# An attention layer with a gated output: eight exponential buffers, a pair's first values one batch later, and filler shared by TensorE's whole batch

## What is computed

```python
xn = layernorm(x)
q, k, v = (xn @ wq.T + bq) * D**-0.5, xn @ wk.T + bk, xn @ wv.T + bv     # by head
s = softmax(q @ k.T + causal_mask) @ v                                   # by head
s = s @ wo.T + bo
g = silu(xn @ weight.T + pooled(xn) @ disha)      # pooled: sums over groups of 64 columns
out = x + s * g
```

## Time and profile before

| | |
|---|---|
| median of 3 runs | 582.64 us (582.53 to 584.64) |
| the profiled execution | 583.26 us |
| its slowest core's span | 581.7 us; the eight cores 575.6 to 581.7 us |
| TensorE busy | 519.4 us, 89% |
| ScalarE busy | 398.0 us, 68% |
| VectorE, GpSimd busy | 222.9 us, 122.1 us |

### The profile page before, as it was taken

The page is one execution under the profiler, slowest core; times in us unless marked ns, Lnnn a source line. Parts: engine busy times, 40 slices in busy tenths (PEclk is TensorE's granted clock), DMA queues, the critical chain, the costliest instruction groups (busy, mean ns, idle before and its releaser), DMA issues.

```text
span 581.7 us, 9555 instructions; the slowest of 8 cores (575.6 to 581.7 us)
## 1 busy us (share of the span) xinstructions
PE 519.4 (89%) x2688; PEld 207.9 (36%) x2688; DVE 222.9 (38%) x335; ACT 398.0 (68%) x495; POOL 122.1 (21%) x157
## 2 busy tenths in 40 slices
PE   2889989889979898899999999999998998999896
PEld 1334433333324343333333333433342333333242
DVE  4447566455311230452022212113110635545625
ACT  2256667767655876787688887677748887888650
POOL 0433332221110211011011111010100332252215
PEclk9989999999989999999999999999999999999899
DMA  7933244043111110111010103110205222223113
GB/s 167 282 105 103 91 145 146 19 154 119 37 37 36 38 55 0 55 38 36 1 38 1 42 32 107 39 37 37 74 0 163 72 91 75 91 73 109 61 50 146
DMA packets 17488, 43.68 MB, mean 75 GB/s; under 512 B 2336, under 2 KB 2336, under 8 KB 17056
## 3 DMA queue, kind: packets, MB, share of 16 engines
q1 hardware_dynamic: 17440, 43.07, 23.7%
HBM read 34.67 MB, written 8.39 MB: 74 GB/s over the span
## 4 chain that ended last, share of the span: by engine, by line
PE 62%; ACT 14%; issue 11%; DVE 8%; DMA 3%; POOL 1%; ACTq 0%; SPq 0%; DVEq 0%; POOLq 0%
PE PSF L556 34%; PE PSS L568 10%; PE PSO L586 10%; ACT PT L732 9%; PE PSO L588 7%; DVE QA L696 2%; DVE QA L695 2%; DMA xfirst<-x 2%; DMA wo_sb<-wo 1%; ACT Rb L742 1%; ACT Rb L741 1%; ACT Rb L744 1%; DVE Vp L638 1%; DVE QA L655 1%; PE PSS L556 1%
## 5 line engine op out<-in xcount | busy, mean ns | idle before, releaser
L732 ACT ACTIVATE PT<-PSS,neg 128x1024 f16<-128x1024 f32 (+1 forms) x320 | 299.3, 982 | 110.0 <-PE PSS L568 106.7
L761 POOL TENSOR_TENSOR PT<-PT,tri_sb 128x256 f16<-128x256 f16 x128 | 88.2, 699 | 424.8 <-ACT PT L732 421.0
L556 PE MATMUL PSF<-XG,wqk 128*128 128x512 f16 x512 | 126.2, 383 | 3.9 <-DVE Vp L638 2.2
L586 PE MATMUL PSO<-PT,Vp 128*128 128x512 f16 (+1 forms) x320 | 111.5, 353 | 11.2 <-DVE QA L696 8.9
L568 PE MATMUL PSS<-QA,KT 64*128 64x512 f16 (+3 forms) x640 | 99.4, 353 | 24.4 <-ACT PT L732 17.7
L588 PE MATMUL PSO<-PT,Vp 128*128 128x512 f16 (+1 forms) x320 | 108.9, 350 | 0.0
L556 PEld LDWEIGHTS PSF<-XG,wqk 128*128 128x128 f16 x512 | 49.0, 98 | 58.6 <-issue 7.0
L638 DVE TENSOR_TENSOR Vp<-PSF,bvb 128x512 f16<-128x512 f32 x32 | 22.1, 691 | 117.7 <-PE PSF L556 117.6
L556 PE MATMUL PSF<-wv_sb,XG 128*128 128x512 f16 x256 | 65.9, 384 | 1.1 <-DVE Vp L638 0.7
L568 PEld LDWEIGHTS PSS<-QA,KT 64*128 64x128 f16 x640 | 27.3, 93 | 109.2 <-issue 107.9
L649 DVE TENSOR_SCALAR KT<-PSF,bqk 128x512 f16<-128x512 f32 x32 | 24.0, 750 | 92.4 <-PE PSF L556 92.1
(11 more groups left out here) (39 smaller groups left out, 268.4 us busy)
## 6 DMA issues: line engine op xcount, KB each, us to landing
wqk<-wqk SPq DMA_DIRECT2D x32, 512.0 KB, 3.4
xin<-x SPq DMA_DIRECT2D x24, 256.0 KB, 3.2
out<-esb SPq DMA_DIRECT2D x24, 256.0 KB, 2.0
wbuf<-wT SPq DMA_DIRECT2D x16, 256.0 KB, 3.3
wv_sb<-wv SPq DMA_DIRECT2D x2, 1024.0 KB, 12.3
wo_sb<-wo SPq DMA_DIRECT2D x1, 2048.0 KB, 8.7
out<-elast SPq DMA_DIRECT2D x8, 256.0 KB, 2.4
xfirst<-x SPq DMA_DIRECT2D x4, 256.0 KB, 4.8
```

What stands on the lines that cost most here:

```text
L556: ins = pe.matmul(ps(n), l, r, start=ec == 0, stop=ec == ECH - 1)
L586: pe.matmul(PSO[:, 0, off:512], Vp[:, sc, p, 0:128], PT[u % 6][:, 0, off:512], start=first, stop=last)
L732: act.activation(PT[u % 6][:, :, off:512], PSS[:, 2 * t[2]:2 * t[2] + 2, off:512], AF.Exp, bias=neg2[:], scale=0.125).then_inc(s_exp, 1)
L761: pool.tensor_tensor(a, a, tri2, ALU.mult).then_inc(s_mask, 1)
```

## The change

- `PT` has eight buffers, `wqk` two; `elast` lies in `QA` alone, and the waits of the `XB` tokens on GpSimd go with it.
- `PV`: in stage 0 none in a pair's first batch and two in its second. In the later stages one, one, none, two in the first four batches, then one each.
- `LNK` stands behind the batch's second exponential; `NRM` is due 2.6 us after it.
- Filler is given so that a batch's own work on TensorE plus its filler is in proportion to its exponentials, with 1.8 us more for the batch before whose exponentials `LNK` stands. `BOUNDARY` is gone; `QUOTA` is unchanged.
- A transpose is put behind up to three tiles so that it ends a batch's filler.

```diff
+                if q[0][0] == "T" and count - done > 3 and put_off[0] < 3 and q[1][0] in "KQV":
+                    q[0], q[1] = q[1], q[0]
+                    put_off[0] += 1
+                    continue
...
                     whole(*w)
-                    done += 2
-                    continue
+                    put_off[0] = 0
+                    return done + 2
...
+    def due_values(tc, i):
+        if tc == 0:
+            return 2 if i == 1 and lag[0] != lag[-1] - 1 else 0
+        return (1, 1, 0, 2)[i] if i < 4 else 1
...
-            act = [sum(0.22 + 2 * (512 - off) * 0.83e-3 for _, _, off in bs[b][2]) for b in mine]
-            extra = 0 if before[0] < 0 else ECH if before in GATES else min(BOUNDARY, 0.45 * max(quota, 0))
-            share = [max(quota - extra, 0) * a / sum(act) for a in act]
+            cols = [sum(512 - off for _, _, off in bs[b][2]) for b in mine]
+            act = [0.44 + 2 * c * 0.83e-3 for c in cols]
+            if before[0] >= 0:
+                act[2 if tc else 0] += 1.8
+            former = [sum(512 - off for _, _, off in bs[b][2]) for b in lag]
+            if tc:
+                did = [former[0], former[1], 0, cols[0] + cols[1]] + cols[2:-2]
+            else:
+                did = [0, sum(former)]
+            own = [c / 2400 + 2 * d / 2400 + 0.2 for c, d in zip(cols, did)]
+            extra = ECH if before in GATES else 0
+            span = sum(own) + MM_US * max(quota - extra, 0)
+            share = [max(span * a / sum(act) - o, 0) for a, o in zip(act, own)]
...
-                if len(lag) > 2:
+                for _ in range(due_values(tc, i)):
...
-                    end = values(lag.pop(0))
+                    end = values(lag.pop(0)) or end
                 order.append(("E", b, 1))
+                if end:
+                    sums(*end)
-                if tc == 3 and (p, i) in ((3, 3), (4, 0), (4, 5), (5, 2), (5, 6), (6, 3), (6, 6), (7, 3)):
+                if tc == 3 and p >= 4 and i in (1, 4):
                     order.append(("XB",) + xb.pop(0))
```

More of the change, by code:

```diff
@@ L106, in evict @@
         order.append(("EV", n) + tiles[n])
-        if kind == "Q" and tiles[n][1] * 8 + tiles[n][2] + 3 < 32:
-            order.append(("WQK", tiles[n][1] * 8 + tiles[n][2] + 3))
+        if kind == "Q" and tiles[n][1] * 8 + tiles[n][2] + 2 < 32:
+            order.append(("WQK", tiles[n][1] * 8 + tiles[n][2] + 2))
         if tiles[n] == ("Q", 3, 7):
@@ L222, in values, with sums @@
         advance(sum(2 * (512 - off) for _, _, off in units) / 2400)
[L223 to L229, removed]
+        return (tc, p) if units[1][1] == 4 * tc + 3 else None
+    def sums(tc, p):
+        k = tc * 8 + p
+        order.append(("LNK", k))
+        if k < 31:
+            later(2.6, "NRM", k)
+    def due_values(tc, i):
+        if tc == 0:
+            return 2 if i == 1 and lag[0] != lag[-1] - 1 else 0
+        return (1, 1, 0, 2)[i] if i < 4 else 1
     xb = [(tt, h) for tt in range(12, 16) for h in range(2)]
@@ L240, in schedule @@
             quota = QUOTA[tc][p] - over
-            act = [sum(0.22 + 2 * (512 - off) * 0.83e-3 for _, _, off in bs[b][2]) for b in mine]
             before = (tc, p - 1) if p else (tc - 1, 7)
-            extra = 0 if before[0] < 0 else ECH if before in GATES else min(BOUNDARY, 0.45 * max(quota, 0))
-            share = [max(quota - extra, 0) * a / sum(act) for a in act]
+            cols = [sum(512 - off for _, _, off in bs[b][2]) for b in mine]
[11 more added lines that the diff above has]
+            share = [max(span * a / sum(act) - o, 0) for a, o in zip(act, own)]
+            share = [x * max(quota - extra, 0) / max(sum(share), 0.01) for x in share]
             due_by, emitted = 0.0, 0
@@ L249, in schedule @@
                 order.extend([("S", b), ("E", b, 0)])
-                advance(sum(512 - off for _, _, off in units) / 2400 + 0.2)
+                advance(cols[i] / 2400 + 0.2)
                 lag.append(b)
                 end = None
-                if len(lag) > 2:
+                for _ in range(due_values(tc, i)):
                     c, r, old = bs[lag[0]]
@@ L279, in schedule @@
         order.append(("MM", n, 0, ECH - 1))
-    values(lag.pop(0))
+    sums(*values(lag.pop(0)))
     for n in last[2:4]:
@@ L341, in build_program @@
     o_wqk = used
-    wqk = [at(f"wqk{i}", [NP, 2, ECH, NP], F16) for i in range(3)]
+    wqk = [at(f"wqk{i}", [NP, 2, ECH, NP], F16) for i in range(2)]
     o_PT = used
-    PT = [at(f"PT{i}", [NP, 2, 512], F16) for i in range(6)]
+    PT = [at(f"PT{i}", [NP, 2, 512], F16) for i in range(8)]
     Rb = [at(f"Rb{i}", [NP, 512], F32) for i in range(2)]
@@ L367, in build_program @@
     xlast = [at(f"xlast{i}", [NP, E], F16, o_wqk + 2048 * i) for i in range(4)]
-    elast = [at(f"elast{i}", [NP, 512], F32, o_wqk + 8192 + 2048 * i if i < 2 else o_QA + 2048 * (i - 2))
-             for i in range(8)]
+    elast = [at(f"elast{i}", [NP, 512], F32, o_QA + 2048 * i) for i in range(8)]
     tlast = [at(f"tlast{i}", [NP, 512], F32, o_PT + 2048 * i) for i in range(6)]
@@ L403, in build_program @@
         s_wo = sem("s_wo")
-        s_wqk = [sem(f"s_wqk{i}") for i in range(3)]
+        s_wqk = [sem(f"s_wqk{i}") for i in range(2)]
         s_wt = [sem(f"s_wt{i}") for i in range(2)]
@@ L443, in sync_program @@
             sp.dma_start(out=tri[:], in_=tri_d).then_inc(s_tri, 16)
-            for c in range(3):
+            for c in range(2):
                 sp.dma_start(out=wqk[c][:], in_=wqk_d[c].rearrange(
@@ L548, in tensor_program @@
                         elif kind == "K":
[L549 removed]
+                            l, r = wqk[(8 * i + j) % 2][:, 0, ec, :], keys(i, ec)
                         elif kind == "Q":
[L551 removed]
+                            l, r = wqk[(8 * i + j) % 2][:, 1, ec, :], keys(i, ec)
                         elif kind == "G":
```

26 lines of the change are left out of this document (13 added, 13 removed).

## The result

The changed kernel takes 594.33 us (median of 4 runs, 593.29 to 596.66) where the kernel before takes 582.64 beside it: a ratio of 1.0195, 95% interval 1.0149 to 1.0241. Forecast were 578.5 us and a range of 567 to 588, so both the direction and the range were wrong.

A forecast was written before the change was run, and what follows sets the result against it. TensorE's work plus some 65 us of its waits was taken to bound the kernel. 25.5 us taken away, 21.0 added and 0.5 of clock turned 583.26 into 579.3, so a median of 578.5 us; range 567 to 588.

The forecast's parts named there:

- (j): TensorE's clock: half a stretch more at 1.2 GHz behind new waits on the slowest core, +0.5 us.
- (b): Scores waiting for exponentials in stages 1 to 3: the new filler shares take away 8 us of 25.4.
- (i): Loads into two `wqk` buffers land in time: 0 us, at most 0.7 once; gate bursts also 0.
- (e): Tiles in the filler wait for a bank, their evictions blocked behind `NRM`, in stages 1 to 3: 10.9 us added.
- (a): A pair's first values, now two batches later, no longer wait for the former pair's normalisation: all 11 us go.
- (c): Stages 0 and 1: a tile straight behind a transpose no longer waits for an eviction; gain 4.6 us.
- (d): Stage 0: one score batch no longer stands right behind its projection; gain 1.7 us.
- (f): Transposes wait for their rows: row block 14 in stage 2 3.7 us, two in stage 0 1.4 each; 6.5 added.
- (g): Start of stage 1: first values wait 2.7 us for `NRM`, where 0.43 is found before; net 2.3 added.
- (h): Stage 1: two LayerNorm activations hold exponentials back, the next pair's scores wait 0.65 us each; 1.3 added.
- The rival that stood on it: The clock falls after every long wait: four times 1.7 us, 584 to 585 us; chance 0.07.
- They cost more: Blocked evictions at pair ends cost more, by a later `NRM` or delayed Q tiles; 587 us at 0.8 each; chance 0.22.

The follow-up runs named there:

- shares_old: The changed kernel with the filler shares (`act`, `extra`, `share`) of the kernel before: 605.17 us.
- nrm_late: The changed kernel with `NRM` due 3.7 us behind `LNK` for 2.6 in stages 1 to 3: 583.85 us, ratio to before 0.9981.
- b_wqk2: The kernel before with two of its three `wqk` buffers, each load issued one Q tile later: 586.34 us, ratio to before 0.9993.
- t_pop: The changed kernel with the next row block's LayerNorm statistics listed as soon as a transpose is done: 583.15 us, ratio to before 0.9982.
- t14_late: Changed kernel, `NRM` at 3.4 us, stage 0's last values a batch later, LayerNorm early except in stage 2: 573.80 us; 570.08 with stage 2 early too.

## Why the prediction was wrong, point by point

Two steps failed. (j) put the clock at +0.5 us where it was 6.8. And the waits, forecast 4.5 us down, went 4.6 up: (b) won too little, (i) and the statistics that the put-off moved were set at nothing. The blocked evictions of (e) were right and made the largest cost.

**(a) Values for `NRM`, -11: right.** The earlier trace rows against the waits of after: the 11.3 us are down to 0.5, apart from the start of stage 1. shares_old has none of them either, so the old shares don't bring them back.

**(b) Exponentials, -8: too large.** By the waits view 25.4 became 21.6 (14.8 and 40 times 0.17), by the distances on TensorE 28.5 became 22.4: 4 to 6 us. Stage 2's regular pairs came as forecast (15.15 for 15.1), stage 3's 0.5 longer (20.51 for 20.0), and there are more of them. shares_old shows that the shares do it. The sign named for it, more waits but of 0.2 us, did not come: 40 waits of 0.54 us on average for 45 of 0.56.

**(c) and (d), -6.3: right.** The 0.94 us behind transposes are gone; at one of the five places the tile, now behind scores, still waits 0.5. The scores' 1.7 us are 0 too.

**(e) Blocked evictions, +10.9: right.** 3.0, 3.6 and 1.05 us in pairs 3, 6 and 4 for 2.8, 2.7 and 0.7; 1.3 us at the V tile of stage 2, 0.75 at a V tile in pair 0 of stage 1 for 0.9; the waits of the two gate tiles grew from 0.6 us to 1.0 and 1.1 where 1.0 more was forecast for each. About 10.7 together. nrm_late takes them away but for the one in pair 0 of stage 1, and in pair 4 of stage 3 a longer wait for `NRM` takes its place.

**(f) Transposes, +6.5: right in place, 1 us short.** 3.8 for 3.7, and 1.7 and 2.1 us for twice 1.4.

**(g), (h): right.** 3.2 for 2.7; 0.9 for 1.3.

**(i) Two wqk buffers, 0: wrong.** The K tile of stage 0 waits 1.5 us on average, up to 2.9. The step took the page's median of 3.4 us for a load's landing and said that SyncE's queue held nothing else there; at this place two `wbuf` loads stand ahead, and the weights landed 4.6 to 7.0 us after issue. On two of the eight cores the eviction that the tile needs came later still, behind such a `wbuf` load in VectorE's order. b_wqk2 shows that the buffers alone cost nothing: its load took up to 6.7 us and still came in time, and it is the order without values between that made the way too short.

**At nothing in the sum: 1.7 us.** The K tile of pair 5 in stage 0 waits behind a Q tile's eviction, `NRM` and statistics: 1.7 us, gone in t_pop. The step that failed is "every added wait is a queue on VectorE or TensorE behind an `NRM` whose place in the list moved": the put-off also moved the next row block's statistics a batch later, which the rows of the order showed at the one place I looked at. And behind two gate bursts, set at 0 by (i), the scores of the batch after the next wait 0.4 and 0.7 us more than before (at 193 and 443 us of core 0), since the table load holds the exponentials back and the batch has no values to cover it; these two are in what (b) measured.

With 0.5 us at the start that no edit touched, these come to 7 to 9 of the 9.1 us: 2 to 4 in (b), 1.1 in (f), 0.5 in (g), 1.5 in (i), 0.5 in (c), 1.7 and 0.5, less 0.2 of (e) and 0.4 of (h). The rest isn't placed. Four cores of either kernel also wait for the load of `wo_sb` in pair 2 of stage 3, 1.3 to 2.1 us before and 1.9 to 2.7 after, which no term names. The last step of the sum has a slip of its own: 579.3 less 0.6 is 578.7.

**(j) The clock, +0.5: wrong, and the costliest step.** It took half a stretch more on the slowest core; there were four more per core, 6.8 us. I had named four waits of 2.7 us and more, which came as 3.0, 3.6, 3.2 and 3.8, and priced them by one wait of the kernel before that was followed on five cores of eight. By the table above such waits have a stretch with them seven times in ten, and over 3.3 us nine in ten. nrm_late removes the waits and the stretches behind them go, and t14_late brings one back with its wait. The rule of the Trainium skill (TensorE: Matmul & The Clock Gate, section "Why this matters for your kernels"), that pauses between bursts bring the clock down, gave 6.8 us; the runs agree with it, and t14_late by itself. The rival that stood on it was given 0.07, and it was right in its mechanism; what it lacked was the 9 us of waits.

**The rivals.** "They cost more" named 587 and slower evictions; the time it gave is the nearest, but its mechanism isn't what happened: the evictions cost what was forecast.

## What to carry to other kernels

A new wait of TensorE of 3 us cost 4.1 here on average, one of 3.8 us 5.2 and up to 5.5: price it with the stretch at 1.2 GHz behind it, and look for the number in the order (here when `NRM` is due, and where the next `LN` is taken up) that makes it shorter than 2 us, where one in four or fewer had a stretch with it. When a planner's rule makes a step end early, list everything that stood behind that step in its queue, at every place where the rule acts. Take a load's landing from the stretch in which it is needed, not from the median of the page.

## What the runs showed of the hardware

Two output operations of VectorE that took 0.69 us each in the earlier trace rows took 1.05 and 1.39 us in nrm_late, at the place where GpSimd's operations for the last rows now stand:

```profile
480.02 1.15 POOL L798 TENSOR_TENSOR elast<-bob,XG 128x512 f32<-128x512 f16 x1 [6.41 <-PE PSF L580]
481.31 1.41 POOL L800 TENSOR_TENSOR elast<-elast,xlast 128x512 f32<-128x512 f32 x1
```

VectorE has two SBUF inputs in its two, and each ends 0.55 us behind GpSimd's (481.72 behind 481.17, 483.28 behind 482.72). All traces together show the same. Of such output operations 4084 started with no GpSimd operation under way, and none took over 0.70 us. 1292 started beside one, and each of them ended 0.54 to 0.64 us behind it, the longest after 1.63 us. The evictions `esb<-PSF`, with one input in PSUM, took 0.69 us in all 904 cases beside GpSimd. The Trainium skill (SBUF — State Buffer, section "Who interferes with whom") says that an operation of VectorE with two SBUF inputs and a GpSimd operation that reads SBUF share a port and one waits for the other; the traces agree.
